# Two GNN layers in one kernel: ScalarE's copies of layer 0 in threes, the work around its last t reordered, two load slots swapped

## The chip, the cores and the metric

The kernel runs on one core of one Trainium2 chip. The time is device microseconds (us) of one execution; three runs are given, and one execution was taken by the hardware profiler. All numbers below are for float32 data.

## What is computed

With `adj` of 5120 x 5120 and `x` of 5120 x 64 (cut to what matters):

```python
# layer 0
u = par_u[0]*par_u[1]*(diag_u[:, None]*x[:2048] @ W_u) + x[:2048]
i = par_i[0]*par_i[1]*(diag_i[:, None]*x[2048:] @ W_i) + x[2048:]
e = concatenate([u, i])
h = adj @ (adj.T @ e)
out = (h - mean(h)) * rsqrt(var(h) + 1e-5) * gamma + beta + x
x = layernorm(x + out)
# layer 1, a Chebyshev filter over the same adj
T1 = adj @ x;  T2 = 2*(adj @ T1) - x;  T3 = 2*(adj @ T2) - T1
x = layernorm(x + x@w[0] + T1@w[1] + T2@w[2] + T3@w[3] + bias)
```

`adj` has 105 MB and doesn't fit on the chip; it is read once in layer 0 and about twice in layer 1.

## The kernel before

**Layer 0 (lines 297 to 1091).** `adj` is read in 20 *panels* of 256 columns. A panel is 5 segments of 1024 rows (1 MB each), loaded by SyncE's queue (SP) into one of two places, the slots 0 and 1. For panel j, TensorE sums t = (panel).T @ e over all rows (`add_t`, L942), 8 recorded matmuls for each of ten *units*, two units per segment. ScalarE takes the sum out of PSUM (L739), two small matmuls combine it (L1002), and ScalarE writes the result, t_cols (L741), which raises the semaphore t_ready. In the pass over panel j+1, TensorE adds panel j's share of h = adj @ t. For that it needs the panel turned, and there are three ways:

- The first three segments in the order of work (k = 0, 1, 2), half of them: six *items* per panel. TensorE transposes four 128x128 blocks (`turn_blocks`, L954) into a PSUM bank, ScalarE copies the bank out (an *eviction*, `copy_turned`, L722), TensorE multiplies (`add_h`, L962). Two banks and two copies exist. The other half of these segments comes as *tiles*: 512x512 pieces of `adj`, loaded a second time by SP in four quarters of 256 KB with pieces of 512 bytes (L321), three tiles per two panels, transposed by VectorE (`turn_tile`, L472) and multiplied at L993 with t_quart, which VectorE makes from t_cols once per two panels (`quarter_t`, 16 small copies, L501).
- Segment k = 3: VectorE transposes it in 32x32 blocks (`turn_across`, L494), and ScalarE moves the blocks to their places in 16 copies of 32x512 (`spread_across`, L732). TensorE multiplies at L982 (`add_h_spread`).
- Segment k = 4: VectorE alone, in 16 transposes of 32x512 (`turn_low`, L484); TensorE multiplies at L970 (`add_h_low`).

Each engine works in the order written. ScalarE's order in a panel is: eviction 0, eviction 1, four copies, eviction 2, four copies, eviction 3, four copies, eviction 4, four copies, eviction 5, then t. The copies wait for turn_across. VectorE's order for two panels is: wait t_ready, quarter_t, turn_across, turn_low, tile 2; wait t_ready, turn_across, turn_low, tiles 0 and 1. So every second pass of TensorE has quarter_t ahead of turn_across; it is called the *late pass* here (t into slot 0), the other the *early pass* (t into slot 1). In the last five groups of two panels VectorE also centres parts of x (`center_xq`), behind tiles 0 and 1. SP's order is: slot 0 k = 0, 1, tile 2, k = 2, 3, 4; slot 1 k = 0, 1, tile 0, k = 2, 3, tile 1, k = 4. A segment's load waits until TensorE has begun the half that frees it (seg_done), or, for k = 3 and 4, until VectorE has turned it.

**Around the last t (L576 to L632, L807 to L826, L1071 to L1091).** After t of the last panel, VectorE does quarter_t, turn_across, the last tile 2, turn_low and then the norm of layer 0 in steps for 5 pieces of h (`norm_step`). ScalarE copies each finished h bank out (`take_h`, L767), TensorE turns and centres it (`turn_h`, L1066), ScalarE squares and copies it (`take_y`, L776 and L778), and ScalarE takes roots (`root`, L784) between VectorE's steps. GpSimd clears two thirds of `terms` once spread and all tiles of layer 0 are used (L394).

**Layer 1 (from L1201).** `adj` is read as pairs of 512x512 tiles of 2 MB, each half by SP and half by ScalarE's queue (L274), into four slots; VectorE transposes a tile (L464), TensorE multiplies it (L1100, L1113, L1151). Slots 0 and 1 lie in the tiles' raw buffers. Slots 2 and 3 lie in the panels' memory: slot 2 over the segments of k = 1, 2 and 3 of slot 1's panel, slot 3 over k = 0, e and turn_low's output; between them lies a buffer for a turned tile. Slot 2's load waits for all transposes of the last panel and for turn_across, slot 3's for TensorE's last use of turn_low's output (low_used).

Of the kernel before, what the change touches and what calls it, by code (L numbers as in the profile page):

```python
# [38 lines left out]
Q32 = 32  # L39
# [15 lines left out]
def resnorm_chebyshev(nc, x, adj, W_u, diag_u, par_u, W_i, diag_i, par_i, gamma, beta, weight, bias, out):  # L55
# [12 lines left out]
    with ExitStack() as ctx:  # L68
# [3 lines left out]
        def sem(name):  # L72
# [40 lines left out]
        pairs = [raw_base[:, 0:pair_size], raw_base[:, pair_size:2 * pair_size], shared[:, at:at + pair_size],  # L113
                 shared[:, at + pair_size + tile_size:at + 2 * pair_size + tile_size]]
        turned += [shared[:, at + pair_size:at + pair_size + tile_size],
# [182 lines left out]
        def _(sp):  # L298
# [48 lines left out]
            for u in range(len(loads)):  # L347
                if u == 2:
                    sp.wait_ge(at_made, NJ * ITEMS)
                    sp.wait_ge(across_made, NJ)  # L350
                elif u == 3:
                    sp.wait_ge(low_used, NJ + 1)
                else:
                    sp.wait_ge(tile_turned, free_after(u) + 1 + RAW)
                for q in (1, 0):
                    load_part(sp, u, q)
# [48 lines left out]
        def _(dve):  # L405
# [129 lines left out]
            def beside_group(m):  # L535

                beside_panel(1, m * 2 + 2, m)
                turn_last_tile(m)
                beside_panel(0, m * 2 + 3, None)
                turn_first_tiles(m + 1)  # L540
# [32 lines left out]
            with dve.Fori(NG - 1 - NG // 2, NG - 1) as m:  # L573
                beside_group(m)
                for k in range(2):
                    center_xq(m * 2 + (k - 2 * (NG - 1 - NG // 2)))  # L576

            dve.wait_ge(t_ready, NJ)
            quarter_t(NG - 1)
            turn_across(1, NJ)  # L580
            turn_tile(2, DMA * NQ * NG, 2, T1 - 1 - TILED)
            turn_low(1, NJ)
# [33 lines left out]
            norm_steps(5)  # L616
            sweep1_tile(0, *first_rows[0])
# [88 lines left out]
        def _(act):  # L706
# [17 lines left out]
            def spread_across(i, j):  # L724
# [4 lines left out]
                if 1 <= i <= NQ:  # L729
                    q = i - 1  # L730
                    for c in range(NQ):
                        last = nc.scalar.copy(spread[Q32 * c:Q32 * (c + 1), :, :, Q32 * q:Q32 * (q + 1)],  # L732
                                              across[Q32 * q:Q32 * (q + 1), :, c, :, :])
                    if i == NQ:
                        last.then_inc(spread_made, 1)
# [14 lines left out]
            keep_t(0, 0)  # L750
            layer0_panel(1, 1)
# [36 lines left out]
            def load_next():  # L788

                u = issued[0]  # L790
                if u == 2:
                    act.wait_ge(at_made, NJ * ITEMS)
                    act.wait_ge(across_made, NJ)
                elif u == 3:
                    act.wait_ge(low_used, NJ + 1)
# [12 lines left out]
            for k, s in enumerate(SEGS):  # L808
                for cc in range(PB):
                    if k < TILED:  # L810
                        copy_turned(k * PB + cc, (NJ - 1) * ITEMS)
                        spread_across(k * PB + cc, NJ)
                    if (k, cc) == (TILED - 1, PB - 1):
                        load_next()
                        load_next()
                    if k >= 1:
                        (take_h, take_y)[cc](k - 1, SEGS[k - 1])
                    if (k, cc) == (NS - 1, PB - 1):
                        take_h(k, SEGS[k])
                    if k >= 3:  # L820
                        root(2 * k - 6 + cc, 2 * GB)
            load_next()
            take_y(NS - 1, SEGS[-1])
# [71 lines left out]
        def _(pe):  # L895
# [110 lines left out]
            def layer0_panel(slot, j, loads, group=None):  # L1006
# [3 lines left out]
                def add(u):  # L1010
# [9 lines left out]
                    if k == ACROSS:  # L1020
                        add_h_spread(1 - slot, cc, j, False)
                    elif k > ACROSS:
                        add_h_low(1 - slot, cc, j, False)
# [291 lines left out]
```

## Time and profile before

| | before |
|---|---|
| median of 3 runs | 1280.37 us (1279.39 to 1280.75) |
| the profiled execution, its own time | 1280.44 us |
| its span, first to last instruction | 1278.6 us |
| mean granted TensorE clock | 0.976 |
| TensorE matmul busy | 1146.8 us (90%) |
| VectorE busy | 907.4 us (71%) |
| ScalarE busy | 355.7 us (28%) |
| DMA | 361.28 MB, mean 283 GB/s |

Engines are PE (TensorE), PEld (its weight loads), DVE (VectorE), ACT (ScalarE), POOL (GpSimd) and SP (SyncE); a q behind the name is the engine's queue of instructions. "idle ... <- X" is time in which the engine had nothing to do until X released it. Matmuls overlap, so the distance between starts tells more than a duration. Layer 0's regular part lasts from about 75 to 528 us of the span, the work around the last t to about 570 us.

### The profile page before, as it was taken

The page shows a single profiled execution, that of the slowest core. Times are in us where ns is not written, and L with a number is a line of the kernel's source. Part 1 is how long each engine was busy: PE and PEld are TensorE (multiplying, and loading weights), DVE is VectorE, ACT ScalarE, POOL GpSimd, SP SyncE. Part 2 cuts the span into 40 slices and gives each one's busy share as a digit, 9 for nine tenths or more (in the row PEclk, how much of TensorE's full clock was granted, in tenths as well). Part 3 has the DMA queues.
Part 4 walks back from the last instruction along what each step waited for, and adds up shares of the span by engine and source line. Part 5 has one row for each costly group of instructions (what it writes and reads, how often), then busy time and mean ns, then how long its engine had stood idle before and what let it go on. Part 6 is the DMA issues. An engine that isn't in the chain of part 4 may idle for free.

```text
span 1278.6 us, 14176 instructions
## 1 busy us (share of the span) xinstructions
PE 1146.8 (90%) x5164; PEld 503.8 (39%) x5164; DVE 907.4 (71%) x950; ACT 355.7 (28%) x633; POOL 62.4 (5%) x98
## 2 busy tenths in 40 slices
PE   4779999999899899889989999999899999689795
PEld 4335444445444454444433333333344444122221
DVE  2566787697777867879777776665576666678784
ACT  1444565456446545640010000000010000011111
POOL 0730000000000000010000000000000000011111
PEclk9989999999999999999999999999999999888998
DMA  8999999999999999579999999999999999999991
GB/s 234 250 281 250 284 300 259 289 280 271 284 269 262 278 285 266 116 153 299 319 272 346 347 333 311 295 309 270 287 264 338 313 328 319 332 308 347 350 353 51
DMA packets 393847, 361.28 MB, mean 283 GB/s; under 512 B 12252, under 2 KB 392452, under 8 KB 393812
## 3 DMA queue, kind: packets, MB, share of 16 engines
q1 hardware_dynamic: 280212, 247.84, 71.2%
q10 hardware_dynamic: 110880, 110.11, 30.2%
q0 software_dynamic: 2720, 2.86, 1.0%
q8 instruction: 22, 0.36, 0.1%
q14 instruction: 13, 0.11, 0.0%
HBM read 359.45 MB, written 1.31 MB: 282 GB/s over the span
## 4 chain that ended last, share of the span: by engine, by line
PE 59%; DVE 14%; ACT 12%; issue 5%; ACTq 4%; SPq 4%; DMA 1%; POOL 0%; DVEq 0%
PE bank L1100 30%; ACT terms L732 9%; PE bank L942 6%; ACTq L274 4%; DVE turned L464 4%; PE bank L1151 4%; PE bank L962 3%; PE bank L970 3%; PE bank L982 3%; DVE t_quart L501 3%; PE bank L1113 3%; DVE terms L494 2%; SPq L332 2%; SPq L321 2%; PE bank L954 1%
## 5 line engine op out<-in xcount | busy, mean ns | idle before, releaser
L1100 PE MATMUL bank<-turned,terms 128*128 128x512 f32 x680 | 301.3, 596 | 3.3 <-DVE turned L464 2.7
L942 PE MATMUL bank<-shared 128*64 128x256 f32 x1600 | 229.2, 390 | 12.6 <-DMA shared<-in_adj 12.6
L484 DVE STREAM_TRANSPOSE shared<-shared 32x512 f32<-32x512 f32 x320 | 224.0, 700 | 4.1
L732 ACT COPY terms<-terms 32x512 f32<-32x512 f32 x320 | 197.1, 616 | 41.5 <-DVE terms L494 37.0
L464 DVE STREAM_TRANSPOSE turned<-shared 128x2048 f32<-128x2048 f32 x70 | 160.7, 2303 | 63.4 <-PE bank L1100 53.0
L464 DVE STREAM_TRANSPOSE turned<-raw 128x2048 f32<-128x2048 f32 x70 | 160.3, 2301 | 55.3 <-PE bank L1100 42.6
L1100 PEld LDWEIGHTS bank<-turned,terms 128*128 128x128 f32 x680 | 126.6, 190 | 168.9 <-issue 165.1
L942 PEld LDWEIGHTS bank<-shared 128*64 128x64 f32 x1600 | 115.8, 138 | 104.5 <-issue 58.8
L962 PE MATMUL bank<-scratch,t_cols 128*64 128x512 f32 x240 | 125.8, 606 | 34.2 <-ACT scratch L722 34.2
L494 DVE STREAM_TRANSPOSE terms<-shared 128x2048 f32<-128x2048 f32 x20 | 46.2, 2311 | 80.9 <-ACT t_cols L741 80.6
L993 PE MATMUL bank<-turned,t_quart 128*64 128x512 f32 x160 | 83.8, 610 | 1.9 <-DVE t_quart L501 1.9
L954 PEld LDWEIGHTS bank<-ident,shared 128*128 128x128 f32 x480 | 51.9, 144 | 72.9 <-issue 57.5
L954 PE MATMUL bank<-ident,shared 128*128 128x128 f32 x480 | 78.4, 287 | 0.4 <-issue 0.4
L722 ACT COPY scratch<-bank 128x512 f32<-128x512 f32 x120 | 70.4, 587 | 25.2 <-PE bank L954 24.1
L833 ACT COPY scratch<-bank 128x512 f32<-128x512 f32 x19 | 11.1, 585 | 224.9 <-PE bank L1100 150.2
L1151 PE MATMUL bank<-turned,terms 128*64 128x512 f32 x224 | 62.3, 602 | 7.2 <-DVE turned L464 7.2
L1113 PE MATMUL bank<-turned,terms 128*64 128x512 f32 x216 | 58.4, 667 | 7.2 <-DVE turned L464 7.2
L501 DVE COPY t_quart<-t_cols 32x64 f32<-32x64 f32 x160 | 33.8, 211 | 39.0 <-ACT t_cols L741 37.0
L982 PE MATMUL bank<-terms,t_cols 128*64 128x512 f32 x160 | 57.7, 605 | 0.0
L399 POOL DMA_DIRECT2D out<-scratch x40 | 21.7, 549 | 687.2 <-DVE scratch L681 687.2
L962 PEld LDWEIGHTS bank<-scratch,t_cols 128*64 128x64 f32 x240 | 29.2, 137 | 65.0 <-ACT scratch L722 53.5
L842 ACT COPY scratch<-bank 64x512 f32<-64x512 f32 x10 | 5.8, 579 | 165.8 <-PE bank L1100 165.8
(142 smaller groups left out, 1035.5 us busy)
## 6 DMA issues: line engine op xcount, KB each, us to landing
shared<-in_adj SPq DMA_DIRECT2D x100, 1024.0 KB, 9.9
raw<-in_adj SPq DMA_DIRECT2D x106, 512.0 KB, 10.4
raw<-in_adj ACTq DMA_DIRECT2D x106, 512.0 KB, 12.5
shared<-in_adj SPq DMA_DIRECT2D x104, 512.0 KB, 10.9
shared<-in_adj ACTq DMA_DIRECT2D x104, 512.0 KB, 12.7
raw<-in_adj SPq DMA_DIRECT2D x120, 256.0 KB, 7.6
xq<-in_x POOLq DMA_DIRECT2D x40, 32.0 KB, 6.9
out<-scratch POOLq DMA_DIRECT2D x40, 32.0 KB, 5.2
```

The lines of the kernel that those rows point to most:

```text
L464: nc.vector.transpose(turned[place].rearrange("p (c b i) -> p b c i", c=GB, i=Q32), part_of[:, all_tiles[n][1] % SPAN]).then_inc(tile_turn ...
L484: last = nc.vector.transpose(low_turned[Q32 * c:Q32 * (c + 1), :, :, Q32 * q:Q32 * (q + 1)], low[Q32 * q:Q32 * (q + 1), :, :, Q32 * c:Q32 ...
L501: last = nc.vector.tensor_copy(t_quart[Q32 * q:Q32 * (q + 1), c * H:(c + 1) * H], t_cols[Q32 * c:Q32 * (c + 1), q // PB, q % PB * H:(q % P ...
L732: last = nc.scalar.copy(spread[Q32 * c:Q32 * (c + 1), :, :, Q32 * q:Q32 * (q + 1)], across[Q32 * q:Q32 * (q + 1), :, c, :, :])
L942: last = nc.tensor.matmul(t_bank[H * odd:H * (odd + 1), 0:PW], e[:, s * SB + b, :], panels[slot][:, s * SB + b, :], start=(k == 0 and b < ...
L954: last = nc.tensor.transpose(turn_bank[i % 2][:, b * P:(b + 1) * P], panels[slot][:, SEGS[k] * SB + b, cc * P:(cc + 1) * P], ident[:, :])
L962: nc.tensor.matmul(h_bank[SEGS[k]][0:H, :], t_cols[:, slot, cc * H:(cc + 1) * H], at_turned[i % AT], start=False, stop=stop, skip_group_ch ...
L982: last = nc.tensor.matmul(h_bank[SEGS[ACROSS]][H * gg:H * (gg + 1), :], t_cols[:, slot, cc * H:(cc + 1) * H], spread[:, cc, gg * GB:(gg + ...
L993: last = nc.tensor.matmul(h_bank[SEGS[k]][H:P, :], t_quart[:, c * H:(c + 1) * H], turned0[k][:, c * BANK:(c + 1) * BANK], start=False, sto ...
L1100: last = nc.tensor.matmul(sum_bank[parity][:, :], terms[:, c * GB + i, columns], turned[place][:, i * BANK:(i + 1) * BANK], start=(first a ...
L1113: last = nc.tensor.matmul(sum_bank[parity][H * odd:H * (odd + 1), :], terms[:, c * GB + i, 2 * H:3 * H], turned[place][:, i * BANK:(i + 1) ...
L1151: last = nc.tensor.matmul(odd_bank[H:P, :] if apart else sum_bank[parity][0:H, :], terms[:, c * GB + i, 0:H], turned[place][:, i * BANK:(i ...
```

## The change

ScalarE's copies are three behind each of evictions 1 to 4 and four behind eviction 5. TensorE adds the share of k = 4 (low) before that of k = 3 (spread) in the panels' passes. ScalarE runs one square root on a column of the identity after the first t. center_xq moves between tile 2 and the early pass's wait for t. Around the last t, VectorE turns tile 2 and the across segment before it waits for the last t, and leaves the last quarter of turn_low until piece 0 of the norm has gone through its five steps; ScalarE's order is written out anew. Slots 2 and 3 of layer 1 change places, with a turned-tile buffer behind them, and wait for other work.

```diff
-        pairs = [raw_base[:, 0:pair_size], raw_base[:, pair_size:2 * pair_size], shared[:, at:at + pair_size],
-                 shared[:, at + pair_size + tile_size:at + 2 * pair_size + tile_size]]
-        turned += [shared[:, at + pair_size:at + pair_size + tile_size],
+        pairs = [raw_base[:, 0:pair_size], raw_base[:, pair_size:2 * pair_size], 
+                 shared[:, at + pair_size:at + 2 * pair_size], shared[:, at:at + pair_size]]
+        turned += [shared[:, at + 2 * pair_size:at + 2 * pair_size + tile_size],
...
                 if u == 2:
+                    sp.wait_ge(at_made, (NJ - 1) * ITEMS + 2 * PB)
+                elif u == 3:
                     sp.wait_ge(at_made, NJ * ITEMS)
                     sp.wait_ge(across_made, NJ)
-                elif u == 3:
-                    sp.wait_ge(low_used, NJ + 1)
...
-            def beside_group(m):
+            def beside_group(m, beside=lambda: None):
 
                 beside_panel(1, m * 2 + 2, m)
                 turn_last_tile(m)
+                beside()
                 beside_panel(0, m * 2 + 3, None)
                 turn_first_tiles(m + 1)
...
             with dve.Fori(NG - 1 - NG // 2, NG - 1) as m:
-                beside_group(m)
-                for k in range(2):
-                    center_xq(m * 2 + (k - 2 * (NG - 1 - NG // 2)))
-
+                def center_two():
+                    for k in range(2):
+                        center_xq(m * 2 + (k - 2 * (NG - 1 - NG // 2)))
+                beside_group(m, center_two)
+
+            turn_tile(2, DMA * NQ * NG, 2, T1 - 1 - TILED)
+            dve.wait_ge(seg_loaded[1][SEGS[ACROSS]], DMA * (NJ // 2))
+            turn_across(1, NJ)
             dve.wait_ge(t_ready, NJ)
             quarter_t(NG - 1)
-            turn_across(1, NJ)
-            turn_tile(2, DMA * NQ * NG, 2, T1 - 1 - TILED)
-            turn_low(1, NJ)
+            turn_low(1, NJ, range(NQ - 1))
...
             norm_steps(5)
+            turn_low(1, NJ, range(NQ - 1, NQ))
             sweep1_tile(0, *first_rows[0])
...
-                if 1 <= i <= NQ:
-                    q = i - 1
-                    for c in range(NQ):
-                        last = nc.scalar.copy(spread[Q32 * c:Q32 * (c + 1), :, :, Q32 * q:Q32 * (q + 1)],
-                                              across[Q32 * q:Q32 * (q + 1), :, c, :, :])
-                    if i == NQ:
-                        last.then_inc(spread_made, 1)
+                blocks = [(q, c) for q in range(NQ) for c in range(NQ)]
+                for q, c in blocks[3 * i - 3:3 * i if i < ITEMS - 1 else len(blocks)] if i else ():
+                    last = nc.scalar.copy(spread[Q32 * c:Q32 * (c + 1), :, :, Q32 * q:Q32 * (q + 1)],
+                                          across[Q32 * q:Q32 * (q + 1), :, c, :, :])
+                if i == ITEMS - 1:
+                    last.then_inc(spread_made, 1)
...
             keep_t(0, 0)
+
+            act.wait_ge(ident_made, 2)
+            nc.scalar.activation(stats[:, 1, 0:1], ident[:, 0:1], ACT.Sqrt)
...
             load_next()
-            for k, s in enumerate(SEGS):
-                for cc in range(PB):
...
             load_next()
+            before = (NJ - 1) * ITEMS
+            copy_turned(0, before)
+            copy_turned(1, before)
+            spread_across(1, NJ)
+            copy_turned(2, before)
+            take_h(0, SEGS[0])
+            spread_across(2, NJ)
+            copy_turned(3, before)
+            take_y(0, SEGS[0])
+            load_next()
+            spread_across(3, NJ)
+            copy_turned(4, before)
+            root(0, 2 * GB)
+            take_h(1, SEGS[1])
+            spread_across(4, NJ)
+            copy_turned(5, before)
+            take_y(1, SEGS[1])
+            load_next()
+            root(1, 2 * GB)
+            spread_across(5, NJ)
+            for k in range(2, TILED + 1):
+                take_h(k, SEGS[k])
+                take_y(k, SEGS[k])
+            take_h(NS - 1, SEGS[-1])
+            for n in range(2, 4):
+                root(n, 2 * GB)
             take_y(NS - 1, SEGS[-1])
...
                     if k == ACROSS:
+                        add_h_low(1 - slot, cc, j, False)
+                    elif k > ACROSS:
                         add_h_spread(1 - slot, cc, j, False)
-                    elif k > ACROSS:
-                        add_h_low(1 - slot, cc, j, False)
```

ScalarE's queue waits and issues slot 2's and slot 3's loads under the same new conditions as SP (`load_next`, not shown twice).

## Rows read from the trace of the kernel before

**Rows 1.** The page's costliest groups: busy us, mean ns, idle before and its releaser.

```profile
L962 PE MATMUL bank<-scratch,t_cols 128*64 128x512 f32 x240 | 125.8, 606 | 34.2 <-ACT scratch L722 34.2
```

**Rows 2.** Chain that ended last, two panels apart: start, length, what.

```profile
432.08 2.32 DVE terms L494
482.02 2.32 DVE terms L494
```

**Rows 3.** PE's timeline, a late pass: start, length, instruction, idle before.

```profile
183.31 0.59 PE L962 MATMUL bank<-scratch,t_cols 128*64 128x512 f32 x1
...
186.94 0.64 PE L962 MATMUL bank<-scratch,t_cols 128*64 128x512 f32 x1 [1.01 <-ACT scratch L722]
...
190.07 0.64 PE L962 MATMUL bank<-scratch,t_cols 128*64 128x512 f32 x1 [0.45 <-ACT scratch L722]
...
193.19 0.64 PE L962 MATMUL bank<-scratch,t_cols 128*64 128x512 f32 x1 [0.44 <-ACT scratch L722]
...
196.32 0.64 PE L962 MATMUL bank<-scratch,t_cols 128*64 128x512 f32 x1 [1.19 <-ACT scratch L722]
```

**Rows 4.** ACT's timeline, the same pass.

```profile
183.79 2.50 ACT L732 COPY terms<-terms 32x512 f32<-32x512 f32 x4 [3.16 <-DVE terms L494]
```

**Rows 5.** PE's timeline, the early pass that follows.

```profile
215.22 0.59 PE L962 MATMUL bank<-scratch,t_cols 128*64 128x512 f32 x1
...
217.68 0.59 PE L962 MATMUL bank<-scratch,t_cols 128*64 128x512 f32 x1
...
220.17 0.64 PE L962 MATMUL bank<-scratch,t_cols 128*64 128x512 f32 x1 [0.60 <-ACT scratch L722]
```

**Rows 6.** DVE's timeline, the late pass: turn_low.

```profile
183.68 11.40 DVE L484 STREAM_TRANSPOSE shared<-shared 32x512 f32<-32x512 f32 x16
```

**Rows 7.** SP's waits from 120 to 170 us: total, times, longest.

```profile
SPq L332 <- PE bank L942: 1.0, 1, 1.0
```

**Rows 8.** SP's waits from 372 to 422 us.

```profile
SPq L332 <- PE bank L942: 25.6, 6, 7.8
```

**Rows 9.** Windows: length, PE busy, PEld, DVE, ACT, POOL, PE clock, DMA share, GB/s.

```profile
112.00:164.00 52.00, 48.32 (x311) 24.18 (x311) 38.67 (x57) 30.01 (x53) 0.00 (x0) 1.00 1.02 273
164.00:216.00 52.00, 48.32 (x312) 24.18 (x310) 38.68 (x56) 30.04 (x52) 0.00 (x0) 1.00 1.09 289
```

**Rows 10.** The page's DMA issues: count, KB each, us to landing.

```profile
shared<-in_adj SPq DMA_DIRECT2D x100, 1024.0 KB, 9.9
...
raw<-in_adj SPq DMA_DIRECT2D x120, 256.0 KB, 7.6
```

**Rows 11.** Line 332, one load: segment k = 4 of panel 5 (counted from 0).

```profile
L332 SPq DMA_DIRECT2D shared<-in_adj x1: 2612/2612/2612, 158.6 to 158.6; - x1
...
DMA to landing us min/median/max: 9.5/9.5/9.5
```

**Rows 12.** Line 332, one load: segment k = 4 of panel 19, the last.

```profile
L332 SPq DMA_DIRECT2D shared<-in_adj x1: 1063/1063/1063, 501.1 to 501.1; - x1
...
DMA to landing us min/median/max: 9.3/9.3/9.3
```

**Rows 13.** PE's timeline: first use of that segment, then around turn_h.

```profile
523.36 1.03 PE L942 MATMUL bank<-shared 128*64 128x256 f32 x8
...
561.87 3.63 PE L1066 MATMUL bank<-centres,scratch 64*64 64x128 f32 x32 [4.86 <-ACT scratch L767]
...
568.35 1.96 PE L1066 MATMUL bank<-centres,scratch 64*64 64x128 f32 x32
```

**Rows 14.** DVE's timeline behind the last t: quarter_t.

```profile
528.76 3.18 DVE L501 COPY t_quart<-t_cols 32x64 f32<-32x64 f32 x16 [2.52 <-ACT t_cols L741]
```

**Rows 15.** A window behind the last load of layer 0: length, clock, DMA share, GB/s.

```profile
515.00:518.00 3.00, 1.00 0.00 0
```

**Rows 16.** ACT's timeline around the last t: the first root.

```profile
553.14 1.28 ACT L784 ACT_TABLE_LOAD   x1
554.44 0.21 ACT L784 ACTIVATE stats<-stats 128x8 f32<-128x8 f32 x1
```

More of the change, by code:

```diff
@@ L791, in load_next @@
                 if u == 2:
+                    act.wait_ge(at_made, (NJ - 1) * ITEMS + 2 * PB)
+                elif u == 3:
                     act.wait_ge(at_made, NJ * ITEMS)
                     act.wait_ge(across_made, NJ)
-                elif u == 3:
-                    act.wait_ge(low_used, NJ + 1)
                 else:
@@ L807, in _ @@
             load_next()
-            for k, s in enumerate(SEGS):
-                for cc in range(PB):
[L810 to L821, printed above, removed]
-            load_next()
+            load_next()
+            before = (NJ - 1) * ITEMS
[24 more added lines that the diff above has]
+                root(n, 2 * GB)
             take_y(NS - 1, SEGS[-1])
```

## The prediction

> **What bounds the kernel now.** I read the page's groups first. TensorE waits 34.2 us at L962 for ScalarE's evictions [rows 1]. The chain of waits shows how regular layer 0 is: two panels take 482.02 - 432.08 = 49.94 us [rows 2]. TensorE's timeline shows where the waits are. In the early pass the multiplications of consecutive items start 217.68 - 215.22 = 2.46 us apart, which is TensorE's own pace for a unit; for item 5, which has one transpose less ahead of it, it is ready about 1.94 us behind item 4, but starts 2.49 behind [rows 5]: 0.55 us lost. In the late pass the starts are 183.31, 186.94, 190.07, 193.19 and 196.32 [rows 3]. Against 2.46, 2.46, 2.46 and 1.94 (and 2.46 between items 1 and 2) the losses are 1.17, 0.67, 0.66 and 1.19 us, 3.7 in all. Their cause is ScalarE's order: the copies can't start before 183.79, when turn_across behind quarter_t is done, and four of them last 2.50 us [rows 4], so an eviction comes every 3.13 us, slower than TensorE's 2.46.
>
> The second thing to read is how far the loads are ahead. SP waits 1.0 us for TensorE between 120 and 170 us [rows 7], but 25.6 us between 372 and 422 [rows 8]: early in layer 0 the queue has no time to spare and TensorE is barely served, later the loads have gained a lead. The kernel of before is thus bound by TensorE and ScalarE, but not by much. Two panels load 10 x 1024 KB and 12 x 256 KB [rows 10], 13.6 MB. In the stretches in which SP hardly waits the DMA moves 273 and 289 GB/s [rows 9]: 13.6 MB take 49.9 and 47.2 us, 48.5 us at the mean of 281. TensorE's 49.94 lies above that, which is why the lead grows.
>
> **The change, part by part.**
>
> *Copies in threes, late pass.* Three copies take 1.88 us. The eviction of item 2 starts at 183.79 + 1.88 instead of + 2.50, and item 2 starts 0.63 us earlier. From there an eviction comes every 1.88 + 0.6 = 2.48 us, TensorE's own 2.46: items 3 and 4 lose nothing. Item 5's eviction ends at 185.67 + 3 x 2.48 + 0.6 = 193.7, so it starts at about 193.8, not 196.32: 2.5 us gained, with 0.6 still lost there.
>
> *Early pass.* Item 5's eviction comes 2 to 3 us earlier, the 0.55 us go.
>
> *Low before spread.* The four copies behind eviction 5 end at 193.7 + 2.5 = 196.2, and spread is now wanted only after two more units. Low is wanted about 1.8 us behind item 5, at 195.5 in the late pass; turn_low ends at 183.68 + 11.40 = 195.08 [rows 6]. The cover is 0.4 us; if it fails, up to that much per late pass comes back. Cost: nothing.
>
> *center_xq moved.* In both places VectorE waits for t with time to spare: nothing in the regular part. At the end it makes room for the tile and the across turned ahead.
>
> *Sum for TensorE.* Nine late passes at 2.5 and nine early ones at 0.55 give 27.5 us, and a pace of 46.9 us for two panels.
>
> *The loads.* At 48.5 us for two panels they are slower than 46.9. That the queue waited little in rows 9 makes 48.5 the pace of a full queue, and the DMA becomes the bound once the lead is used up. The lead at panel 5's last segment: it lands at 158.6 + 9.5 = 168.1 [rows 11], and TensorE uses it at about 173.8, seven pairs of 49.94 before the last panel's use at 523.36 [rows 13]. By then TensorE has gained two late and two early passes, 6.1 us, more than the lead of 5.7. So from panel 5 on the loads set the time. The last segment, seven pairs on, lands at 168.1 + 7 x 48.5 = 507.6 and is used at once; before it landed at 501.1 + 9.3 = 510.4 [rows 12] and was used at 523.36. **Layer 0 gains 15.8 us**, not 27.5. The bounds: at 47.2 us the last segment would land at 498.5 (gain 24.9), at 49.9 at 517.4 (gain 6.0).
>
> Here a page speaks the other way. The Trainium skill (DMA: Bandwidth & Descriptors, "Where 436 GB/s comes from") puts the limit of reads from HBM at about 358 GB/s per core. By it 13.6 MB take 38 us and the loads would never bind; no stretch of layer 0 in rows 9 comes near it, so the trace speaks against it here. What it would give is the second rival below.
>
> *Tile 2 and across ahead of quarter_t.* Before, the last tile had landed by 515 us [rows 15], long ahead of its use. With the loads as the bound it is issued behind the last segment and lands 515 - 510.4 = 4.6 us after it. VectorE now stands in line for it: transposing takes 2.3 us, across 2.3 (a transpose of this size is 2.32 in rows 2), quarter_t 3.2 [rows 14], so quarter_t ends 12.4 us after the last segment. Before it ended at 531.94, 8.6 us after 523.36. **Loss 3.8 us**: t_quart comes at 520.0, 11.9 us earlier than before. ScalarE's second load_next waits for the same tile, under the same cover. If the loads aren't the bound, VectorE is late here by half a microsecond only.
>
> *From t_quart to layer 1's first tiles.* Before, TensorE stands idle 4.86 us for take_h, and the turn_h behind it takes 3.63 us where a later one takes 1.96 [rows 13]. ScalarE loads the root's table for 1.28 us [rows 16], on the path; VectorE and with it the second root wait for that. After, the table is loaded after the first t, where TensorE stands still for the DMA of panel 1's segments anyway, the roots of piece 0 don't wait for turn_low's last quarter, and h is taken out between fewer copies. 4.86 + 1.7 = 6.5 us can go. A new wait comes: the last four copies (2.5 us) are behind the second root, and TensorE needs them after item 5: about 2 us. **Gain 4.5 us**, bounds 1.3 (the table alone) and 6.5.
>
> The Trainium skill (ScalarE: Activation LUTs, "What ACT_TABLE_LOAD costs") adds 1.38 us of drain to the 1.28 of a load. Here the root starts at 554.44, 0.02 us after the load ends [rows 16]; with the page's drain the gain would be 1.4 larger, by the trace it isn't.
>
> *Slots 2 and 3.* Their loads are issued earlier. Layer 1's first 20 tiles are bound by TensorE and VectorE, and four slots fill in any case: nothing. Everything behind is shifted.
>
> **Sum**, against the profiled execution's 1280.44 (0.07 above the median): -15.8 + 3.8 - 4.5 = -16.5, **1263.9 us**.
>
> **The rivals.**
>
> 1. *Loads slower in a full queue*, 49.2 to 50.5 us for two panels: at 49.9 the gain in layer 0 is 6.0, in all 6.7: 1273.7. For it: the stretch of 273 GB/s [rows 9]. Against: it is followed by 289.
> 2. *TensorE stays the bound* (the page's limit, or loads that flow better when the queue is less full): -27.5 + 0.5 - 4.5 = -31.5, 1248.9. For it: nothing waits for the DMA late in layer 0 [rows 8]. Against: rows 7, a queue with no pause at a slower pace than 46.9. Values between this and the forecast belong to it: 47.2 gives -25.6, 1254.8.
> 3. *Slower.* Place: the loads of layer 0. Above a certain pace the last segment lands later than it was used before. With 3.8 lost and 4.5 gained behind it, the change is even when it lands at 524.1, which is (524.1 - 168.1) / 7 = 50.9 us for two panels or 268 GB/s; at 51.5 us it gives 1284.9. Faster TensorE and closer loads would have to cost each other more than any stretch of rows 9 shows.
> 4. *No effect*: low's cover of 0.4 us fails wholly and a wait moves from item 2 to low. It would return 0.4 to 2.5 us per late pass; for no gain it must return all. Against: across and low start when they did.
>
> **How the numbers follow.** The forecast with the loads as the bound at 48 to 49.2 us (1260 to 1269): 0.56. Rival 2, with what lies between: 0.24. Rival 1: 0.14. Rivals 3 and 4: 0.03 each. 0.2%, 2.6 us, is about what a measurement of this kernel can tell. Faster by more: 0.94; within: 0.03; slower: 0.03. The range 1251 to 1272 takes in the forecast, most of rival 2 and half of rival 1: 0.82.
>
> **What would show it.** Right: TensorE's idle at L962 falls from 34.2 us to under 15 and its idle at L942 for DMA rises, at k = 4 of the slot-1 panels; two panels take 48 to 49 us; SP's waits stay under 5 us in every 50; VectorE waits for a raw tile's DMA just before the last across; evictions of the late pass come 2.5 us apart; the table load stands near 37 us. Wrong: SP's waits grow again as in rows 8 and the pair takes 46.9 (rival 2); TensorE waits at L970 for turn_low (rival 4); or the last segment is used later than 515 (rival 1).

## The result and the profile after

The changed kernel takes 1266.41 us (median of four runs, 1263.03 to 1267.96) against 1280.39 us; the ratio is 0.9889, with a 95% interval of 0.9875 to 0.9902. The profiled execution took 1265.37 us with a span of 1263.5, 15.1 us less than before. The forecast was 1263.9 us, 2.5 below the median.

The page's groups after, as in [rows 1]; the lines have moved, L960 is L942 of before, L980 is L962:

```profile
L960 PE MATMUL bank<-shared 128*64 128x256 f32 x1600 | 231.3, 393 | 23.1 <-DMA shared<-in_adj 23.0
...
L980 PE MATMUL bank<-scratch,t_cols 128*64 128x512 f32 x240 | 125.9, 606 | 10.9 <-ACT scratch L726 10.9
...
L472 DVE STREAM_TRANSPOSE turned<-raw 128x2048 f32<-128x2048 f32 x20 | 45.5, 2299 | 9.8 <-DMA raw<-in_adj 9.4
```

TensorE's idle time for the evictions fell from 34.2 us to 10.9. In its place it now waits 23.0 us for the loads of panels. PE's timeline of a late pass, the answer to [rows 3]:

```profile
178.55 0.59 PE L980 MATMUL bank<-scratch,t_cols 128*64 128x512 f32 x1
...
181.56 0.64 PE L980 MATMUL bank<-scratch,t_cols 128*64 128x512 f32 x1 [0.39 <-ACT scratch L726]
...
184.07 0.63 PE L980 MATMUL bank<-scratch,t_cols 128*64 128x512 f32 x1
...
186.57 0.59 PE L980 MATMUL bank<-scratch,t_cols 128*64 128x512 f32 x1
...
188.92 0.64 PE L980 MATMUL bank<-scratch,t_cols 128*64 128x512 f32 x1 [0.46 <-ACT scratch L726]
...
190.69 0.59 PE L988 MATMUL bank<-shared,t_cols 128*64 128x512 f32 x1
```

The items start 3.01, 2.51, 2.50 and 2.35 us apart, 10.37 in all where it was 13.01. The last line is the first use of low. In the early pass that follows, item 5 now starts 1.72 us behind item 4, where it was 2.49 [rows 5]:

```profile
210.28 0.59 PE L980 MATMUL bank<-scratch,t_cols 128*64 128x512 f32 x1
...
212.00 0.59 PE L980 MATMUL bank<-scratch,t_cols 128*64 128x512 f32 x1
```

VectorE's and ScalarE's timelines of the late pass, turn_low (as [rows 6]) and the last four copies:

```profile
178.93 11.41 DVE L484 STREAM_TRANSPOSE shared<-shared 32x512 f32<-32x512 f32 x16
```

```profile
188.89 2.50 ACT L735 COPY terms<-terms 32x512 f32<-32x512 f32 x4
```

turn_low ends at 190.34, 0.35 us ahead of its use. Where the time goes instead is seen in the early pass, and again at the last segment and the first tiles of layer 1 (PE's timeline):

```profile
215.64 1.08 PE L960 MATMUL bank<-shared 128*64 128x256 f32 x8 [0.89 <-DMA shared<-in_adj]
...
505.55 1.44 PE L960 MATMUL bank<-shared 128*64 128x256 f32 x8 [2.24 <-DMA shared<-in_adj]
...
518.50 2.43 PE L1011 MATMUL bank<-turned,t_quart 128*64 128x512 f32 x4 [2.02 <-DVE t_quart L501]
...
540.37 1.97 PE L1000 MATMUL bank<-terms,t_cols 128*64 128x512 f32 x4 [2.18 <-ACT terms L735]
542.27 2.64 PE L1084 MATMUL bank<-centres,scratch 64*64 64x128 f32 x32
...
550.84 1.98 PE L1118 MATMUL bank<-turned,terms 128*128 128x512 f32 x4 [1.10 <-POOL terms L394]
```

The stop is at k = 4 of slot 1's panels. Line 332 of one load, that segment of panel 5 and of panel 19, the answers to [rows 11, 12]:

```profile
L332 SPq DMA_DIRECT2D shared<-in_adj x1: 2519/2519/2519, 158.4 to 158.4; - x1
...
DMA to landing us min/median/max: 9.6/9.6/9.6
```

```profile
L332 SPq DMA_DIRECT2D shared<-in_adj x1: 1052/1052/1052, 495.7 to 495.7; - x1
...
DMA to landing us min/median/max: 9.8/9.8/9.8
```

They land at 168.0 and 505.5 and are used at once: 337.5 / 7 = 48.2 us for two panels. VectorE's timeline around the last t:

```profile
510.88 2.31 DVE L472 STREAM_TRANSPOSE terms<-raw 128x2048 f32<-128x2048 f32 x1 [6.26 <-DMA raw<-in_adj]
513.12 2.27 DVE L494 STREAM_TRANSPOSE terms<-shared 128x2048 f32<-128x2048 f32 x1
515.31 3.13 DVE L501 COPY t_quart<-t_cols 32x64 f32<-32x64 f32 x16
```

VectorE stands 6.26 us for the last tile, and quarter_t behind it. The difference in three stretches, from the first instruction to the last segment's use, on to the end of t_quart, on to layer 1's first tile:

| us | before | after | difference | forecast |
|---|---|---|---|---|
| last segment used | 523.36 | 505.55 | -17.8 | -15.8 |
| to the end of t_quart | 8.6 | 12.9 | +4.3 | +3.8 |
| to layer 1's first tile | 34.5 (566.44) | 32.4 (550.84) | -2.1 | -4.5 |
| to the end of the span | 712.2 | 712.7 | +0.5 | 0 |
| sum | | | -15.1 | -16.5 |

### The profile page after: what moved, and what is told of

Its sections match the earlier page's. It is cut to its first block, busy times and chain, and to the rows that moved or that the text cites. A ratio compares the mean times of both kernels' runs of the same rounds, so it can differ in the third digit from the quotient of the medians.

```text
span 1263.5 us, 14169 instructions
## 1 busy us (share of the span) xinstructions
PE 1144.8 (91%) x5155; PEld 503.7 (40%) x5164; DVE 903.3 (71%) x950; ACT 353.7 (28%) x634; POOL 62.4 (5%) x98
## 4 chain that ended last, share of the span: by engine, by line
PE 44%; SPq 35%; DVE 8%; issue 4%; ACTq 4%; DMA 3%; ACT 1%; POOL 1%; DVEq 0%; POOLq 0%
PE bank L1118 29%; SPq L321 18%; SPq L332 16%; DVE turned L464 4%; PE bank L1169 4%; ACTq L274 4%; PE bank L1131 3%; DMA shared<-in_adj 3%; DVE xq L464 1%; PE bank L1147 1%; DVE shared L464 1%; PE bank L1274 1%; DMA raw<-in_adj 1%; PE bank L1084 1%; PE bank L1141 1%
## 5 line engine op out<-in xcount | busy, mean ns | idle before, releaser
L960 PE MATMUL bank<-shared 128*64 128x256 f32 x1600 | 231.3, 393 | 23.1 <-DMA shared<-in_adj 23.0
L464 DVE STREAM_TRANSPOSE turned<-raw 128x2048 f32<-128x2048 f32 x70 | 160.3, 2301 | 55.3 <-PE bank L1118 42.6
L960 PEld LDWEIGHTS bank<-shared 128*64 128x64 f32 x1600 | 115.4, 138 | 119.1 <-issue 55.1
L980 PE MATMUL bank<-scratch,t_cols 128*64 128x512 f32 x240 | 125.9, 606 | 10.9 <-ACT scratch L726 10.9
L494 DVE STREAM_TRANSPOSE terms<-shared 128x2048 f32<-128x2048 f32 x20 | 46.2, 2309 | 46.8 <-ACT t_cols L744 46.5
L501 DVE COPY t_quart<-t_cols 32x64 f32<-32x64 f32 x160 | 32.3, 202 | 49.1 <-ACT t_cols L744 47.0
L988 PE MATMUL bank<-shared,t_cols 128*64 128x512 f32 x160 | 57.9, 619 | 0.0
L472 DVE STREAM_TRANSPOSE turned<-raw 128x2048 f32<-128x2048 f32 x20 | 45.5, 2299 | 9.8 <-DMA raw<-in_adj 9.4
```

Source lines behind the costliest of these rows:

```text
L464: nc.vector.transpose(turned[place].rearrange("p (c b i) -> p b c i", c=GB, i=Q32), part_of[:, all_tiles[n][1] % SPAN]).then_inc(tile_turn ...
L960: last = nc.tensor.matmul(t_bank[H * odd:H * (odd + 1), 0:PW], e[:, s * SB + b, :], panels[slot][:, s * SB + b, :], start=(k == 0 and b < ...
L980: nc.tensor.matmul(h_bank[SEGS[k]][0:H, :], t_cols[:, slot, cc * H:(cc + 1) * H], at_turned[i % AT], start=False, stop=stop, skip_group_ch ...
```

## The experiments

The columns "last segment", "to t_quart" and "to first tile" are the same three stretches in each run's own trace, "pace" is the mean time for two panels from panel 5's last segment to panel 19's, both at their use; in parentheses behind the last stretch stands how much of it TensorE lost to its lower clock, an estimate: its busy time times the share of the clock that was not granted, summed over windows of half a microsecond.

| run | us, median (lowest to highest) | pace | last segment | to t_quart | to first tile (low clock) |
|---|---|---|---|---|---|
| before | 1280.39 | 50.1 | 523.4 | 8.6 | 34.5 (1.7) |
| after | 1266.41 (1263.0 to 1268.0) | 48.2 | 505.6 | 12.9 | 32.4 (3.3) |
| e1 | 1276.93 (1275.6 to 1279.9) | 50.1 | 522.4 | 8.6 | 32.3 (1.7) |
| e2 | 1262.15 (1256.7 to 1268.6) | 49.2 | 510.6 | 10.3 | 32.4 (2.0) |
| e3 | 1262.96 (1256.0 to 1270.5) | 48.2 | 505.3 | 10.3 | 30.9 (1.7) |
| e4 | 1267.85 (1258.6 to 1271.4) | 49.2 | 510.6 | 12.2 | 32.1 (3.0) |
| e6 | 1264.39 (1255.3 to 1267.7) | 49.0 | 509.0 | 10.3 | 30.9 (1.7) |
| e7 | 1264.08 (1255.6 to 1268.3) | 49.5 | 512.6 | 10.2 | 31.9 (1.5) |
| e8 | 1267.92 (1257.8 to 1271.0) | 49.6 | 513.1 | 12.3 | 30.7 (1.5) |
| e9 | 1249.40 (1249.2 to 1252.4) | 46.8 | 493.7 | 8.9 | 33.1 (2.7) |
| e10 | 1280.63 (1277.3 to 1282.1) | 50.1 | 522.3 | 8.6 | 35.4 (2.8) |
| e11 | 1269.70 (one run) | 49.2 | 511.3 | 12.3 | 31.4 (1.7) |
| e12 | 1261.93 (one run) | 48.2 | 504.4 | 12.6 | 31.9 (2.8) |
| e13 | 1267.71 (one run) | 48.3 | 508.1 | 12.7 | 30.9 (1.7) |

**e1, the copies in fours again in the panels.** Based on the changed kernel:

```diff
-                for q, c in blocks[3 * i - 3:3 * i if i < ITEMS - 1 else len(blocks)] if i else ():
+                per = 3 if at_end else 4
+                for q, c in blocks[per * i - per:per * i if i < ITEMS - 1 else len(blocks)] if i else ():
...
-                if i == ITEMS - 1:
+                if i == (ITEMS - 1 if at_end else NQ):
...
-                        add_h_low(1 - slot, cc, j, False)
+                        add_h_spread(1 - slot, cc, j, False)
                     elif k > ACROSS:
-                        add_h_spread(1 - slot, cc, j, False)
+                        add_h_low(1 - slot, cc, j, False)
```

> The changed kernel with ScalarE's copies in fours and spread before low in the panels of layer 0 again; everything around the last t stays changed. Theory (the loads bind layer 0 after the change, and its gain is nearly all of the whole): the period of two panels goes back to 49.9 us, SP's waits for TensorE to some 25 us in 50, TensorE's idle time at the evictions to 30 us or more, and the last segment is used at 523 us. VectorE no longer waits for the last tile. 1275 to 1279 us, the rest being what the work around the last t gives by itself. Rival (the gain is mostly made around the last t): 1268 us or less.

Measured 1276.93 us, ratio 0.9982 (0.9971 to 0.9992). SP's waits from 372 to 422 us are those of [rows 8] again:

```profile
SPq L332 <- PE bank L961: 25.5, 6, 7.7
```

So the panels make nearly all of the gain; the work around the last t alone is worth 2.2 us in the trace (34.5 to 32.3) and about 2.3 in the times. The new order has a cost here that neither the forecast nor the expectation has: ScalarE issues four loads in a row ahead of its first evictions (3.96 us in ScalarE's timeline), and TensorE waits for the first eviction until 532.31, 1.4 us beyond the end of t_quart (PE's timeline).

```profile
527.61 3.96 ACTq L274 DMA_DIRECT2D raw<-in_adj  x4
```

```profile
532.31 0.75 PE L981 MATMUL bank<-scratch,t_cols 128*64 128x512 f32 x1 [3.41 <-ACT scratch L726]
```

**e2, the copies in threes alone.** The kernel of before with these two hunks of the change, and nothing else:

```diff
-                if 1 <= i <= NQ:
-                    q = i - 1
-                    for c in range(NQ):
...
+                blocks = [(q, c) for q in range(NQ) for c in range(NQ)]
+                for q, c in blocks[3 * i - 3:3 * i if i < ITEMS - 1 else len(blocks)] if i else ():
...
                     if k == ACROSS:
-                        add_h_spread(1 - slot, cc, j, False)
-                    elif k > ACROSS:
                         add_h_low(1 - slot, cc, j, False)
+                    elif k > ACROSS:
+                        add_h_spread(1 - slot, cc, j, False)
```

> The kernel of before with only the copies in threes and low before spread in the panels. Theory: two panels in 48.2 to 48.6 us, last segment used at 505 to 508 us on landing, SP hardly waits. VectorE keeps its old order, quarter_t first, so t_quart ends 8.6 us behind the last segment, at 514 to 516, not 12.9; from there the old path of 34.5 us. 1262 to 1265 us: as fast as the whole change. Rival (the work around the last t gives the 3 to 5 us that were forecast even with the tile late): 2 us or more slower than the changed kernel.

Measured 1262.15 us, ratio 0.9852 (0.9812 to 0.9893). The last segment is used on landing, but at 510.61, later than expected, and t_quart ends 10.3 us behind it and not 8.6; the last section says why. PE's timeline:

```profile
510.61 1.11 PE L941 MATMUL bank<-shared 128*64 128x256 f32 x8 [2.78 <-DMA shared<-in_adj]
...
553.28 1.98 PE L1099 MATMUL bank<-turned,terms 128*128 128x512 f32 x4
```

In this trace the old order around the last t is thus no slower than the new one once the loads bind: 42.7 us from the last segment to the first tile, where the changed kernel has 45.3. The rival, which had 2 us or more for the new order, falls.

**e3, across first and tile 2 behind quarter_t.** Based on the changed kernel:

```diff
-            turn_tile(2, DMA * NQ * NG, 2, T1 - 1 - TILED)
             dve.wait_ge(seg_loaded[1][SEGS[ACROSS]], DMA * (NJ // 2))
             turn_across(1, NJ)
             dve.wait_ge(t_ready, NJ)
             quarter_t(NG - 1)
+            turn_tile(2, DMA * NQ * NG, 2, T1 - 1 - TILED)
...
-            load_next()
             before = (NJ - 1) * ITEMS
...
             copy_turned(2, before)
+            load_next()
             take_h(0, SEGS[0])
```

> The changed kernel, but around the last t VectorE does across, waits for t, then quarter_t and only then tile 2; ScalarE's second load stands behind eviction 2. Theory (the last tile, which lands late now, holds up quarter_t by 4.3 us and TensorE's clock falls in that wait): t_quart ends 8.6 to 9 us behind the last segment, layer 1's first tile starts 4 to 6 us earlier against the last segment than in the changed kernel; 1259 to 1262 us. Rival (ScalarE's queue or the tile itself sets the end of this stretch): within 1 us of the changed kernel.

Measured 1262.96 us, ratio 0.9885 (0.9829 to 0.9940). In its trace the two panels took 48.2 us, as in the changed kernel's. VectorE's timeline:

```profile
504.20 2.27 DVE L494 STREAM_TRANSPOSE terms<-shared 128x2048 f32<-128x2048 f32 x1
512.39 3.18 DVE L501 COPY t_quart<-t_cols 32x64 f32<-32x64 f32 x16 [5.93 <-ACT t_cols L744]
515.61 2.31 DVE L472 STREAM_TRANSPOSE terms<-raw 128x2048 f32<-128x2048 f32 x1
```

VectorE waits for t now, not for the tile, and t_quart ends at 515.57 instead of 518.44, 10.3 us behind the last segment and not the 8.6 to 9 expected; the last section says why. The first tile starts at 546.48, 41.2 us behind the last segment against 45.3: 4.1 us, inside what was expected of the stretch. The time is 1 us above what was expected. The edit moves one of ScalarE's loads as well as the tile, so the 4.1 us are the worth of both together.

**e4, the changed kernel again.**

> The changed kernel once more, on the chip and in the rounds of the others, since its four runs lie 4.9 us apart where those of before lie 1.4 apart. Theory (bound by loads, its time follows the DMA's pace): again 1263 to 1268 us with the last segment used within 0.1 us of landing. Rival: the spread was chance, and the runs lie within 1.5 us.

Measured 1267.85 us, seven runs from 1258.61 to 1271.41: wider than expected. The kernel of before lay between 1277.32 and 1281.45 in the same rounds. The last segment lands at 510.5 and is used at 510.62.

**e6, e7, e8: e3's, e2's and the changed kernel in common rounds.**

> The version with across, t, quarter_t, tile 2 once more, with more rounds, beside the changed kernel and the copies alone. Theory: 4 us less from the last segment's use to layer 1's first tile than the changed kernel (41 us against 45), so its median is 3 to 5 us below that kernel's, and it is 1 to 2 us ahead of the copies alone; all three vary by 5 us or more with the DMA's pace. Rival: their intervals can't be told apart and neither can the stretches in the traces.

> The kernel of before with the copies in threes and low first, with more rounds. Theory: 42 to 43 us from the last segment's use to layer 1's first tile, so 2 to 3 us below the changed kernel in the median and 1 to 2 above the version with the tile behind quarter_t. Rival: above the changed kernel.

> The changed kernel in the same rounds. Theory: 44 to 46 us from the last segment's use to layer 1's first tile, a median of 1264 to 1268 us, runs spread over 5 us or more.

Ratios: e6 0.9863 (0.9834 to 0.9891), e7 0.9863 (0.9835 to 0.9892), e8 0.9882 (0.9850 to 0.9914). e6's median is 3.5 us below e8's, as expected; e7's is 3.8 below, more than the 2 to 3 expected, and not above e6's. The intervals overlap: as times the three aren't told apart, nor is e6 ahead of e7. e8 reached its first tile 43.0 us behind the last segment, less than the 44 expected, e7 42.1, e6 41.1. The stretch stands in that order in all seven traces (changed 45.3, 44.3, 43.0; e2's 42.7, 42.1; e3's 41.2, 41.1), though with 0.3 us between the changed kernel's shortest and e2's longest. The gain of e3's order over the changed kernel is 3.0 us in the mean. The whole doesn't show it, because the place of the last segment alone moves by 8 us.

**e9, fewer bytes.** Based on the changed kernel; the four quarters of tiles 0 and 1 of layer 0 load half their rows:

```diff
-            def load_layer0_tile(k, last, column):
+            def load_layer0_tile(k, last, column, blocks=slice(0, 16)):
...
-                    sp.dma_start(raw[k][Q32 * q:Q32 * (q + 1), :].rearrange("p (b c) -> p b c", c=P),
-                                 tile_rows[2 * SEGS[k] + 1][:, :, bass.ds(column + P * q, P)])\
+                    sp.dma_start(raw[k][Q32 * q:Q32 * (q + 1), :].rearrange("p (b c) -> p b c", c=P)[:, blocks],
+                                 tile_rows[2 * SEGS[k] + 1][:, blocks, bass.ds(column + P * q, P)])\
...
-                load_panel(1, pair - 1, end - PW, [(k, (pair - 1) * TILED + (k - TILED), end - BANK)
+                load_panel(1, pair - 1, end - PW, [(k, (pair - 1) * TILED + (k - TILED), end - BANK, slice(0, 8))
```

> The changed kernel, but in layer 0 from the second group on the quarters of tiles 0 and 1 load 8 of their 16 blocks of rows, 128 KB instead of 256 (the other half keeps older rows, so h is another one; every engine's work stays). 13.6 MB for two panels become 12.6. Theory (the DMA sets the pace of layer 0): the period of two panels falls from 48.2 us to TensorE's own, 46.5 to 47.2, TensorE no longer waits for k = 4 of the slot-1 panels, SP's waits for TensorE grow in the course of layer 0 as they did before the change, the last segment is used at 494 to 500 us, the whole takes 1247 to 1257 us, and the runs lie closer together. Rival (something else that TensorE waits for, turn_low or the evictions, holds the period at 48.2): the last segment is used at 504 or later.

Measured 1249.40 us, ratio 0.9774 (0.9749 to 0.9799). TensorE's waits from 60 to 510 us, the changed kernel first and this one second (total, times, longest):

```profile
PE bank L960 <- DMA shared<-in_adj: 20.5, 9, 8.2
PE bank L980 <- ACT scratch L726: 8.7, 17, 2.1
```

```profile
PE bank L980 <- ACT scratch L726: 13.8, 17, 3.7
PE bank L960 <- DMA shared<-in_adj: 8.6, 1, 8.6
```

The one wait for a load that is left is the start's. SP's waits from 372 to 422 us in this run, against none in the changed kernel's:

```profile
SPq L332 <- PE bank L960: 29.3, 7, 7.8
```

The pace is 46.8 us, TensorE's own by the forecast's sum (46.9); the last segment is used at 493.7, just ahead of what was expected. No engine's work was changed, only 7.7% of the bytes of two panels. This is the run that shows the bound.

**e10, the same cut in the kernel of before.**

> The same cut of the loads in the kernel of before (h is again another one). Theory: it was bound by TensorE and ScalarE, so the period stays 49.9 us, the last segment is used at 522 to 524 us, the time is within 1.5 us of before; SP's waits only grow earlier. Rival (the loads cost TensorE's neighbours something through the memory too): 3 us or more faster.

Measured 1280.63 us, ratio 1.0004 (0.9990 to 1.0018), with the last segment used at 522.3: there the bytes cost nothing.

**e11, the table late.** Based on the changed kernel:

```diff
             keep_t(0, 0)
-
-            act.wait_ge(ident_made, 2)
-            nc.scalar.activation(stats[:, 1, 0:1], ident[:, 0:1], ACT.Sqrt)
```

> The changed kernel without the square root after the first t, so that the table is loaded at the first root after the last t. Theory (the forecast's term): the table's 1.28 us are on the path: the stretch from the end of t_quart to layer 1's first tile is 33.2 to 33.7 us instead of 32.4. Rival (TensorE's work hides it, since take_h behind the root has about a microsecond to spare): 32.4 within 0.4. The time itself tells nothing at this size.

```profile
537.63 1.28 ACT L787 ACT_TABLE_LOAD   x1
538.92 0.21 ACT L787 ACTIVATE stats<-stats 128x8 f32<-128x8 f32 x1
```

The load is at the first root again, and the stretch is 31.4 us, inside neither expectation and not longer than in the changed kernel's three traces (32.4, 32.1, 30.7). But those differ by their low clock. The part from item 4 to the first tile passed at full clock in e11 and in e8, and there the two can be compared (windows of e11 first, then of e8):

```profile
536.00:555.00 19.00, 14.70 (x131) 7.44 (x129) 10.14 (x17) 14.19 (x35) 4.37 (x1) 1.00 1.02 202
```

```profile
538.00:556.00 18.00, 14.20 (x129) 7.41 (x128) 9.90 (x15) 12.63 (x34) 4.30 (x1) 1.00 1.02 209
```

It takes 17.3 us in e11 (537.66 to 554.97) and 16.8 in e8 (539.34 to 556.12), and e11 has a wait that e8 lacks (PE's timeline):

```profile
542.21 0.64 PE L977 MATMUL bank<-scratch,t_cols 128*64 128x512 f32 x1 [0.53 <-ACT scratch L726]
```

So the table costs about 0.5 us of its 1.28 in this order: most of it is hidden, not all. It is one trace against one.

**e12, slots 2 and 3 as before.** Based on the changed kernel, with the old places and conditions:

```diff
-                 shared[:, at + pair_size:at + 2 * pair_size], shared[:, at:at + pair_size]]
-        turned += [shared[:, at + 2 * pair_size:at + 2 * pair_size + tile_size],
+                 shared[:, at:at + pair_size], shared[:, at + pair_size + tile_size:at + 2 * pair_size + tile_size]]
+        turned += [shared[:, at + pair_size:at + pair_size + tile_size],
...
                 if u == 2:
-                    act.wait_ge(at_made, (NJ - 1) * ITEMS + 2 * PB)
-                elif u == 3:
                     act.wait_ge(at_made, NJ * ITEMS)
                     act.wait_ge(across_made, NJ)
+                elif u == 3:
+                    act.wait_ge(low_used, NJ + 1)
...
             take_y(0, SEGS[0])
-            load_next()
...
             take_h(NS - 1, SEGS[-1])
+            load_next()
```

SP's conditions for slots 2 and 3 are changed in the same way.

> The changed kernel with slots 2 and 3 of layer 1 in their old places and under their old conditions (spread and low stay as changed). Theory: slot 3's load is issued 10 us or more later, and neither TensorE nor VectorE waits for it; from layer 1's first tile to the end the same as in the changed kernel within 1.5 us. Rival: VectorE waits for the pair at tile 6 or 7 and the stretch behind the first tile is 2 us or more longer.

From the first tile to the end 711.2 us (1260.1 - 548.85), 1.4 less than the changed kernel's profiled 712.7; before has 712.2. VectorE waits for no pair between 540 and 650 us in either. The swap costs and brings nothing that shows.

**e13, spread before low.** The changed kernel with TensorE's order of before in the panels, the second half of e1's diff:

```diff
                     if k == ACROSS:
-                        add_h_low(1 - slot, cc, j, False)
-                    elif k > ACROSS:
                         add_h_spread(1 - slot, cc, j, False)
+                    elif k > ACROSS:
+                        add_h_low(1 - slot, cc, j, False)
```

> The changed kernel with spread before low again in the panels; the copies stay in threes. In the changed kernel's late pass TensorE adds low at 190.69 us, where turn_low ended at 190.38, and the last four copies end at 191.39. Theory (the swap only keeps TensorE from waiting for the copies): TensorE waits about 0.7 us for L735 in each late pass, 5 to 8 us in all, and none of it is seen in the time, since the loads set the pace: the last segment is still used on landing, at 504 to 513 us. Rival (without the swap the wait is on the path): the last segment is used with 0.5 us or more behind its landing, and two panels take 0.7 us longer than the loads.

The waits of PE's weight loads from 120 to 500 us hold the line

```profile
PEld bank L1000 <- ACT terms L735: 4.1, 8, 0.5
```

0.5 us in each of eight late passes, a little less than expected, and the last segment is still used within 0.1 us of its landing. So the order of low and spread is cover that the loads' bound makes superfluous; with TensorE as the bound it would be worth some 4 us. That was not run.

## Why the forecast held, and where it didn't

*The copies in threes* did what the working said: item 5 comes 10.37 us behind item 1, the forecast had 10.5, and the early pass loses nothing at item 5 any more. Together with low first they bring TensorE's pace to 46.8 us where the loads let it (e9).

*Low before spread* cost nothing, with a cover of 0.35 us where 0.4 was worked out.

*The loads become the bound.* This was the step that decided, and it held: SP waits for TensorE nowhere from 170 to 470 us, and e9 and e10 speak against the other explanations that were raised: the same cut of the loads gives 17 us after the change (1266.4 to 1249.4) and nothing before it. The forecast's first rival (loads at 49.2 us and more) and the forecast are both to be seen: the changed order met 48.2 to 49.6 us in different executions, where 48.5 was taken from rows of before. At 48.2 the last segment came 2.0 us earlier than forecast, at 49.6 5.5 us later. What was missing is that this pace isn't one number. Before, TensorE's pace hid it, and the runs lay 1.4 to 6 us apart; now each execution's own pace is in its time, and the changed kernel's 17 runs reach from 1257.8 to 1271.4. That the total came within 2.5 us of the forecast is in part luck: in the profiled execution layer 0 gained 2.0 us more than forecast, and the stretch behind t_quart 2.4 less. One reading of the working was off without harm: panel 5's last segment was used at 172.84 and not at about 173.8, since seven pairs of panels took 50.07 us in the mean and the pair in rows 2 took 49.94; the lead was 4.7 us, not 5.7. Rival 2, TensorE still the bound, is what e9 brings about: 1249.4 us, and its 1248.9 was worked out; the agreement hides that e9 gained 29.7 us up to the last segment, not 27.5, and 1.4 from t_quart to the first tile, not 4.5. In the changed kernel itself it doesn't occur: 13.6 MB in 48.2 us are 283 GB/s with the queue never waiting. The Trainium skill (DMA: Bandwidth & Descriptors, "Where 436 GB/s comes from") gives a limit of about 358 GB/s per core. The trace speaks against it as the mean pace of these loads; only while segments land do windows of 2 us come near it, as the last section shows.

*Tile 2 ahead of quarter_t*: t_quart came 4.3 us later against the last segment where 3.8 were forecast; VectorE could begin on the tile 5.3 us behind the segment (510.88), not 4.6. But the order's own cost is smaller. The versions with quarter_t first (e2, e3, e6, e7) have 10.2 to 10.3 us and not 8.6, by the lower clock that the last section shows, so the order costs 2.6 us in the first trace and about 2.0 in e4 and e8.

*From t_quart to the first tile* is the step that failed, by its size: 2.1 us were gained, not 4.5. Its term of 6.5 us was TensorE's wait of 4.86 and 1.7 for the turn_h behind it, which ran slowly. That slow turn_h was TensorE at its lower clock, as these windows say (before, then the changed kernel):

```profile
561.00:566.00 5.00, 4.13 (x36) 3.44 (x36) 4.35 (x8) 1.41 (x6) 0.01 (x1) 0.66 0.14 26
```

```profile
541.00:545.00 4.00, 4.00 (x38) 2.56 (x36) 3.70 (x4) 0.04 (x1) 0.00 (x0) 0.66 1.13 218
```

The wait of 4.86 went, but the 1.7 did not: the clock fell again, behind the wait for t_quart and behind the new wait for the four copies, and cost 3.3 us. The rest is waits, and the balance closes:

| us, between the end of t_quart and the first tile | before | after | forecast of the difference |
|---|---|---|---|
| wait for take_h ahead of the fourth turn_h | 4.86 | 0 | -4.86 |
| other waits for evictions and take_h | 2.78 | 0.63 | none |
| wait for the four copies behind the root | 0 | 2.18 | +2 |
| wait for GpSimd's clearing of `terms` | 0 | 1.10 | none |
| lost to the lower clock (estimate) | 1.7 | 3.3 | -1.7 |
| sum | 9.3 | 7.2 | -4.5 |

The clearing starts when spread is used up and ends at 550.8; the wait for it was not taken away to test it. In the forecast the table's 1.28 us were no term beside these, but a part of the wait of 4.86; e11 puts them at 0.5 in the new order. The table of runs supports the part of the clock: the stretch without its loss is 32.8 and 32.7 us in before and e10, 29.1 to 29.2 in all three traces of the changed kernel and in e3, e6, e12 and e13, though the stretches themselves lie between 30.7 and 32.4. So the new order is worth 3.7 us here, and the clock takes 1.6 of them away in the profiled execution, 1.3 in e4, and gives 0.2 in e8. e1 and e9 have 30.6 and 30.4; they hold 1.4 and 1.3 us of waiting for the first eviction more. No run holds the clock up to test this.

*The slots*: nothing that shows, as forecast (e12). No run takes *center_xq*'s new place back by itself.

Of the versions that the loads bind, the one that has both the copies in threes and e3's order has the shortest way from the last segment to the first tile; its times (1262.96 and 1264.39) are not told apart from the copies alone.

## What to carry to other kernels

When a wait between two engines is removed, compare the pace that they then reach with the pace of the queue that feeds them while it has no time to spare. That pace can be read before the change in the stretch in which the queue's own waits are near zero, and the new period is the longer of the two. And work pulled ahead of a wait, because its data have always been there, takes over the wait of its data once the loads are the bound: order by what will land last then, not by what landed first before. And work that was slow at TensorE's lower clock behind a wait isn't gained with that wait, as long as another wait takes its place.

## What the runs showed beside this

TensorE's wait of 2.24 us for the last segment is followed by a slower clock: windows of the changed kernel and of the kernel before over the same work (length, busy times, PE clock, DMA share, GB/s):

```profile
505.00:510.00 5.00, 4.45 (x22) 2.22 (x24) 0.00 (x0) 0.00 (x0) 0.00 (x0) 0.66 1.04 216
518.00:524.00 6.00, 5.50 (x14) 1.84 (x14) 5.85 (x11) 0.59 (x1) 0.00 (x0) 0.72 1.10 342
```

```profile
523.00:528.00 5.00, 5.00 (x34) 2.17 (x31) 2.94 (x7) 0.37 (x1) 0.00 (x0) 1.00 0.60 136
```

From the last segment's use t takes 7.1 us to t_cols instead of 5.4: a mean of 0.66 is a stretch partly at 1.2 and partly at 2.4 GHz. In e2, e3, e6 and e7, where quarter_t waits for t, this is the 1.7 us by which t_quart comes later than 8.6. So a wait for a load at the end of layer 0 costs more than its length. It isn't certain each time: the wait of 2.18 us for the four copies is followed by a lower clock in the changed kernel's trace, e3, e4 and e6, and by none in e1, e8, e9, e12 and e13. What decides it these traces don't show.

The loads' pace in a full queue differs between executions of one program, 48.2 to 49.6 us for the same 13.6 MB. What sets the difference stays open. What makes the mean of about 280 GB/s is seen in windows of 2 us of the kernel before (length, PE clock, DMA share, GB/s):

```profile
186.00:188.00 2.00, 1.00 1.10 348
...
194.00:196.00 2.00, 1.00 1.10 198
```

The first lies where segments of 1 MB are landing, with pieces of 1 KB; the second where the quarters of a tile are, issued from 186.62 to 194.64 and landed some 8 us later, with pieces of 512 bytes to 32 partitions each. The DMA engines are busy in both. So the tiles' 23% of the bytes cost more than their share of the time, which fits that e9's cut of 7.7% of the bytes was enough. Whether it is the size of the pieces or the number of partitions was not tried.
